# Expert blocks of 128 rows and two lookup tables in a two-layer ViT tower

## What is computed

```python
h = tok(x)                                # patch embedding, 128 x 3 x 224 x 224
h = h + causal_attention(layernorm(h))
h = h + ffn0(layernorm(h))                # top 2 of 32 experts, hidden size 128, relu
h = h + decayed_mix(layernorm(h))
h = h + ffn1(layernorm(h))                # top 2 of 16 experts, hidden size 512, gelu

# ffn0, with w zero except for a token's two chosen experts:
h = relu(einsum('td,edh->teh', xt, keys))
out = einsum('teh,te,ehv->tv', h, w, values)
```

## Time and profile before

| What | us |
|---|---|
| Median of 3 runs | 1412.7 (1410.9 to 1418.58) |
| Profiled execution, its own time | 1420.37 |
| Its span | 1418.6 |
| Front, tables and pads of L0 | 0 to 489 |
| Expert blocks of L0 | 489 to 746 |
| Middle | 746 to 1054 |
| Expert blocks of L1 | 1054 to 1343 |
| End | 1343 to 1418.6 |

### The profile page before, as it was taken

How to read it: one execution, slowest core, us unless ns; L and a number is a source line. 1 busy time by engine, 2 the same in 40 slices (tenths; PEclk the granted TensorE clock), 3 DMA queues, 4 the chain that set the end, 5 groups by cost and what they waited for, 6 DMA issues and landing times.

```text
span 1418.6 us, 23674 instructions
## 1 busy us (share of the span) xinstructions
PE 995.0 (70%) x6272; PEld 821.7 (58%) x6272; DVE 810.1 (57%) x2985; ACT 501.7 (35%) x1416; POOL 707.3 (50%) x698
## 2 busy tenths in 40 slices
PE   5999999999985066666643544444429999999700
PEld 3576666766654055555533444444419999999700
DVE  1577878778775033333325777777625666666433
ACT  1443434434332011111113444444415665665400
POOL 1034535445353267777770566666654555555500
PEclk9999999999985598888865777766659999999955
DMA  9756666566311654444424333333257777777388
GB/s 374 265 196 225 217 231 228 200 231 220 120 40 30 189 156 146 145 142 144 146 61 106 97 96 97 91 91 72 55 162 252 249 241 244 243 248 244 98 240 237
DMA packets 121170, 243.61 MB, mean 172 GB/s; under 512 B 21976, under 2 KB 88603, under 8 KB 114754
## 3 DMA queue, kind: packets, MB, share of 16 engines
q1 hardware_dynamic: 83168, 189.90, 41.3%
q0 software_dynamic: 21504, 34.73, 7.8%
q10 hardware_dynamic: 16458, 18.51, 4.6%
HBM read 188.84 MB, written 60.18 MB: 176 GB/s over the span
## 4 chain that ended last, share of the span: by engine, by line
PE 54%; DMA 13%; DVE 11%; issue 7%; ACT 5%; POOL 5%; SPq 3%; ACTq 0%; DVEq 0%; POOLq 0%
PE ps L654 11%; PE ps L639 8%; PE ps L491 7%; PE ps L488 5%; DMA xin<-resid_L 4%; PE ps L733 4%; POOL results_L L1578 4%; DMA results_L<-xin 4%; DMA xin<-lists_L 3%; PE ps L736 3%; ACT ntok L994 2%; PE ps L552 2%; PE ps L570 2%; PE ps L536 2%; PE ps L624 2%
## 5 line engine op out<-in xcount | busy, mean ns | idle before, releaser
L1565 POOL DMA_INDIRECT lists_L<-rows,slots x320 | 358.3, 1120 | 417.2 <-issue 374.1
L1578 POOL DMA_INDIRECT results_L<-xin x352 | 344.6, 979 | 217.7 <-DVE xin L1384 145.5
L654 PEld LDWEIGHTS ps<-xin,hTb 128*128 128x128 f32 x1664 | 219.7, 200 | 9.2 <-DVE hTb L1353 0.3
L654 PE MATMUL ps<-xin,hTb 128*128 128x128 f32 x1664 | 224.2, 282 | 0.1
L491 PE MATMUL ps<-xin,w_emb 128*128 128x512 f32 x384 | 180.8, 603 | 10.3 <-DMA w_emb<-in_w_main 10.3
L624 PE MATMUL ps<-ident,xin 128*128 128x128 f32 x352 | 82.4, 321 | 131.3 <-DMA xin<-lists_L 130.6
L936 ACT ACTIVATE hTb<-ps,xin 128x256 f32<-128x256 f32 x320 | 125.6, 475 | 107.2 <-PE ps L639 107.2
L1353 DVE TENSOR_SCALAR hTb<-ps 128x256 f32<-128x256 f32 x96 | 40.8, 425 | 174.3 <-PE ps L635 174.3
L733 PE MATMUL ps<-ntok,w_emb 104*104 104x128 f32 x160 | 49.2, 432 | 120.2 <-ACT ntok L994 120.2
L624 PEld LDWEIGHTS ps<-ident,xin 128*128 128x128 f32 x352 | 42.7, 154 | 152.4 <-DMA xin<-lists_L 152.3
L810 ACT ACTIVATE xTb<-ps 128x256 f32<-128x256 f32 x96 | 36.9, 384 | 236.6 <-PE ps L624 236.6
(11 more groups left out here) (187 smaller groups left out, 2015.2 us busy)
## 6 DMA issues: line engine op xcount, KB each, us to landing
xin<-in_x_main SPq DMA_DIRECT2D x48, 1536.0 KB, 8.4
xin<-in_w_L SPq DMA_DIRECT2D x80, 578.0 KB
xin<-lists_L SPq DMA_DIRECT2D x176, 132.0 KB
xin<-results_L SPq DMA_DIRECT2D x32, 520.0 KB
xin<-in_w_L SPq DMA_DIRECT2D x96, 128.0 KB
resid_L<-htok ACTq DMA_DIRECT2D x32, 260.0 KB
xin<-resid_L SPq DMA_DIRECT2D x32, 260.0 KB
results_L<-xin POOLq DMA_INDIRECT x352
```

What stands on the lines that cost most here:

```text
L654: mm = pe.matmul(o, hTb[p2][:, f, q * 128:(q + 1) * 128], w2[:, f * D:(f + 1) * D], start=(f == 0), stop=(f == l.FC - 1))
L1565: pool.indirect_dma_start(out=lists[l.name], out_offset=bass.IndirectOffsetOnAxis(ap=slots[h][:, t, k:k + 1], axis=0), in_=rows[h][:, t, k ...
L1578: pool.indirect_dma_start(out=results[l.name], out_offset=bass.IndirectOffsetOnAxis(ap=xblk[u][:, q, PLACE:PLACE + 1].bitcast(U32), axis=0 ...
```

## The change

Blocks of L0 have 128 rows in place of 256. The number of blocks is no longer rounded up to a multiple of 8: L0 has 161, L1 still 80. `rounds` now runs the first 8 blocks, 18 turns of a loop (blocks 8 to 151) and the last 9 (L1: 8) as straight code, on every engine. The semaphore counts that L1 starts from are kept for each buffer, since buffer 0 is used 21 times in L0 and the others 20 times. In place of `tb.entry` there are two tables, `tb.weights_at` with the first row of the expert's weights and `tb.rows_at` with the first row in the lists; SP loads one number from each and divides nothing. VectorE makes them with one instruction less. The buffers in SBUF are the same 8. With 128 rows a block needs one transpose, one scatter and half the columns in each matmul and each copy; its weights are 128 KB as before, its rows 66 KB.

```diff
-        most = (TOKENS * TOP + experts * (block - 1)) // block
+        self.blocks = (TOKENS * TOP + experts * (block - 1)) // block
         self.unroll = unroll
-        self.blocks = -(-most // unroll) * unroll
+        self.rounds = self.blocks // unroll
+        self.turns = [len(range(u, self.blocks, unroll)) for u in range(unroll)]
-L0 = Layer(1, "L0", 32, 128, 256)
+L0 = Layer(1, "L0", 32, 128, 128)
 L1 = Layer(2, "L1", 16, 512, 256)
@@ rounds
-            for u in range(l.unroll):
-                body(u, 0)
-            with eng.Fori(1, l.blocks // l.unroll) as j:
-                for u in range(l.unroll):
+            U = l.unroll
+            for i in range(U):
+                body(i, 0)
+            with eng.Fori(1, l.rounds - 1) as j:
+                for u in range(U):
                     body(u, j)
+            for i in range(U * (l.rounds - 1), l.blocks):
+                body(i % U, i // U)
@@ load, on SP
                 i = l.unroll * j + u
-                entry = sp.value_load(tb.entry[0:1, bass.ds(i, 1)], min_val=0, max_val=l.E * l.step - 1)
-                e, r = entry // l.step, entry % l.step
-
-                sp.wait_ge(k.y_out[u], k.y0 + 16 * l.Q * j)
-                sp.dma_start(wblk[u][:, 0:l.W], weights[bass.ds(e * 128, 128), :]).then_inc(k.blk_in[u], 16)
+                e = sp.value_load(tb.weights_at[0:1, bass.ds(i, 1)], min_val=0, max_val=(l.E - 1) * 128)
+                r = sp.value_load(tb.rows_at[0:1, bass.ds(i, 1)], min_val=0, max_val=l.E * l.room)
+                sp.wait_ge(k.y_out[u], k.y0[u] + 16 * l.Q * j)
+                sp.dma_start(wblk[u][:, 0:l.W], weights[bass.ds(e, 128), :]).then_inc(k.blk_in[u], 16)
@@ tables, on DVE
-                link(dve.tensor_scalar(tb.ef[:, 0:n], pair[0][0:1, 0:n], float(E - 1), None, ALU.min))
+                link(dve.tensor_scalar(tb.weights_at[:, 0:n], pair[0][0:1, 0:n], float(E - 1), 128.0, ALU.min, ALU.mult))
-                link(dve.tensor_scalar(tb.rf[:, 0:n], tb.rf[:, 0:n], float(E * l.room), None, ALU.min))
-                dve.scalar_tensor_tensor(tb.entry[:, 0:n], tb.ef[:, 0:n], float(l.step), tb.rf[:, 0:n],
-                                         ALU.mult, ALU.add).then_inc(T.tables_ready, 1)
+                dve.tensor_scalar(tb.rows_at[:, 0:n], tb.rf[:, 0:n], float(E * l.room), None, ALU.min)\
+                    .then_inc(T.tables_ready, 1)
```

More of the change, by code:

```diff
@@ L65, in __init__ @@
         self.room = TOKENS + block
-        self.step = experts * self.room + 1
-        most = (TOKENS * TOP + experts * (block - 1)) // block
+        self.blocks = (TOKENS * TOP + experts * (block - 1)) // block
         self.unroll = unroll
-        self.blocks = -(-most // unroll) * unroll
+        self.rounds = self.blocks // unroll
+        self.turns = [len(range(u, self.blocks, unroll)) for u in range(unroll)]
         self.W = 2 * hidden + (self.FC + D if self.FC > 1 else 0)
-L0 = Layer(1, "L0", 32, 128, 256)
+L0 = Layer(1, "L0", 32, 128, 128)
 L1 = Layer(2, "L1", 16, 512, 256)
@@ L118, in __init__ @@
         self.cb, self.ge, self.v = sb("t_cb", [32, 1]), sb("t_ge", [32, 192]), sb("t_v", [32, 2])
-        self.ef, self.rf = sb("t_ef", [1, 192]), sb("t_rf", [1, 192])
-        self.entry = sb("t_entry", [1, 192], I32)
+        self.rf = sb("t_rf", [1, 192])
+        self.weights_at, self.rows_at = sb("t_weights_at", [1, 192], I32), sb("t_rows_at", [1, 192], I32)
         self.fr = sb("t_fr", [1, 32], I32)
@@ L166, with __init__ @@
 class BlockSignals:
-    def __init__(self, sem, i0, j0, y0, first=None):
-        self.i0, self.j0, self.y0 = i0, j0, y0
+    def __init__(self, sem, before=None, first=None):
+        self.i0 = before.blocks if before else 0
+        self.j0 = before.turns if before else [0] * NB
+        self.y0 = [16 * before.Q * j0 if before else 0 for j0 in self.j0]
         if first is None:
@@ L343, in build @@
         S = {l.name: LayerSignals(sem, halves, l.name) for l in (L0, L1)}
-        K = {"L0": BlockSignals(sem, 0, 0, 0)}
-        K["L1"] = BlockSignals(sem, L0.blocks, L0.blocks // NB, 16 * L0.Q * L0.blocks // NB, K["L0"])
+        K = {"L0": BlockSignals(sem)}
+        K["L1"] = BlockSignals(sem, L0, K["L0"])
         m_in = halves("m_in")
@@ L385, in rounds, with beyond @@
         def rounds(eng, l, body):
-            for u in range(l.unroll):
-                body(u, 0)
-            with eng.Fori(1, l.blocks // l.unroll) as j:
-                for u in range(l.unroll):
+            U = l.unroll
[3 more added lines that the diff above has]
+                for u in range(U):
                     body(u, j)
+            for i in range(U * (l.rounds - 1), l.blocks):
+                body(i % U, i // U)
+        def beyond(l, u, j, n):
+            return isinstance(j, int) and l.unroll * j + u + n >= l.blocks
         def pads(eng, l, half):
@@ L452, in _ @@
             for u in range(NB):
-                sp.wait_ge(K["L0"].y_out[u], 16 * L0.Q * L0.blocks // L0.unroll)
+                sp.wait_ge(K["L0"].y_out[u], 16 * L0.Q * L0.turns[u])
             for h in range(2):
@@ L462, in _ @@
             for u in range(NB):
-                sp.wait_ge(K["L1"].y_out[u], K["L1"].y0 + 16 * L1.Q * L1.blocks // L1.unroll)
+                sp.wait_ge(K["L1"].y_out[u], K["L1"].y0[u] + 16 * L1.Q * L1.turns[u])
             for h in range(2):
@@ L621, in t1 @@
                     b, jj = turn(u, n, j)
-                    pe.wait_ge(k.blk_in[b], 32 * (k.j0 + jj + 1))
+                    pe.wait_ge(k.blk_in[b], 32 * (k.j0[b] + jj + 1))
                     for q in range(l.Q):
@@ L659, in i_par @@
                     return (u + n) % 2
-                rounds = l.blocks // U
                 t1(0, 0, 0)
@@ L664, in expert_blocks, with step @@
                 t2(0, 0, 0)
-                def step(u, j, last):
-                    if not (last and u + 2 >= U):
+                def step(u, j):
+                    if not beyond(l, u, j, 2):
                         t1(u, j, 2)
-                    if not (last and u + 1 >= U):
+                    if not beyond(l, u, j, 1):
                         t2(u, j, 1)
                     t3(u, j, 0)
[L672 to L678, removed]
+                rounds(pe, l, step)
             def step(g, h, j, ahead_a, ahead_e):
@@ L942, in high @@
                     i = U * j + u + n
-                    act.wait_ge(k.blk_in[(u + n) % U], 32 * (k.j0 + j + (u + n) // U + 1))
+                    act.wait_ge(k.blk_in[(u + n) % U], 32 * (k.j0[(u + n) % U] + j + (u + n) // U + 1))
                     if not (isinstance(i, int) and i < 2):
@@ L952, in expert_blocks, with step @@
                         f(0, 0, n)
-                for u in range(U):
+                def step(u, j):
                     for f, lead in works:
[L955 to L958, removed]
+                        if not beyond(l, u, j, lead):
                             f(u, j, lead)
[L960 to L963, removed]
+                rounds(act, l, step)
             pads(act, L0, 1)
@@ L1311, in tables @@
                 E, n = l.E, l.blocks
-                st = Steps(9 * (l.turn - 1))
+                st = Steps(8 * (l.turn - 1))
                 def link(ins):
@@ L1332, in tables @@
                 dve.wait_ge(T.tab_ps, l.turn)
-                link(dve.tensor_scalar(tb.ef[:, 0:n], pair[0][0:1, 0:n], float(E - 1), None, ALU.min))
+                link(dve.tensor_scalar(tb.weights_at[:, 0:n], pair[0][0:1, 0:n], float(E - 1), 128.0, ALU.min, ALU.mult))
                 link(dve.scalar_tensor_tensor(tb.rf[:, 0:n], iotaB[0:1, 0:n], float(l.block), pair[1][0:1, 0:n],
                                               ALU.mult, ALU.add))
-                link(dve.tensor_scalar(tb.rf[:, 0:n], tb.rf[:, 0:n], float(E * l.room), None, ALU.min))
-                dve.scalar_tensor_tensor(tb.entry[:, 0:n], tb.ef[:, 0:n], float(l.step), tb.rf[:, 0:n],
-                                         ALU.mult, ALU.add).then_inc(T.tables_ready, 1)
-                assert st.n == 9, st.n
+                dve.tensor_scalar(tb.rows_at[:, 0:n], tb.rf[:, 0:n], float(E * l.room), None, ALU.min)\
+                    .then_inc(T.tables_ready, 1)
+                assert st.n == 8, st.n
             tables(L0)
@@ L1374, in gated @@
                     dve.wait_ge(k.y_ps, k.i0 + i + 1)
-                    dve.wait_ge(k.y_out[u], k.y0 + 16 * l.Q * j)
+                    dve.wait_ge(k.y_out[u], k.y0[u] + 16 * l.Q * j)
                     y = ps[:, 6 + p2, 0:l.Q * D].rearrange("p (q d) -> p q d", q=l.Q)
@@ L1378, in gated @@
                     if l.FC > 1:
-                        dve.tensor_tensor(yblk[u][:, :, :], y,
+                        dve.tensor_tensor(yblk[u][:, 0:l.Q, :], y,
                                           wblk[u][:, None, l.W - D:l.W].to_broadcast([128, l.Q, D]), ALU.add)\
@@ L1382, in gated, with step @@
                         dve.wait_ge(y_biased, i + 1)
-                        y = yblk[u][:, :, :]
```

(8 more changed lines are left out.)

## The result

The changed kernel takes 1558.5 us (median of 4 runs, 1557.2 to 1559.0), the kernel before 1412.3 in the same comparison: 1.102 times as long, 95% interval 1.099 to 1.106, or 146 us more. The profiled execution took 1557.2 us, its span 1555.4.

The account below looks back on a forecast made before the run. POOL's scatters were taken to bind before, SP after: 394.2 us of its issuing and the edges end L0's blocks 143 us later; with 1 us for L1, 144 us on the median 1412.7 give 1557 us (1530 to 1590).

Parts of the forecast that it names:

- What binds before: L0's blocks in the kernel before: POOL's scatters bind at 2.55 us per block, SP second at 1.88.
- (e): SP in L0's blocks: two lookups make 2.48 us per block in the loop, 2.18 in straight code; SP binds, 394.2 us.
- (f): Both ends of L0's blocks: smaller pads let SP start 3 us sooner; tail 9.2 us in place of 19.4.
- (g): L1's 80 blocks: the second lookup fits in SP's waits, except 1 us (0 to 2) at the start.
- The sum: Whole kernel: L0's last results land at 889.0 against 746.0, 143 us later, plus 1 us for L1: 1557 us.
- a sign of being wrong: Outside L0's blocks: the prediction is wrong if the rest of the kernel moves by more than some 3 us.
- (a) to (d): L0's POOL (205.6 us), PE, DVE and ACT, buffer loop (1.3 us per block), transfers (105 GB/s): none binds after.
- The 1.3 us of the loop through a buffer: L0: loading, computing, scattering and reloading a buffer takes 7.9 us, over 6 blocks 1.3 us each; not on the path.
- Rival four: L0's blocks: not slower, SP does not bind; POOL or the buffer loop does at 1.3 us; about 1372 us, chance 3%.
- Overlapping lookups: SP in L0: the second lookup overlaps the first, adding 0.3 us in place of 0.68; about 1498 us, chance 7%.
- Dearer lookups: SP in L0: at 567 ns per load, two loads add 0.58 us per block, 93 us; about 1650 us, chance 6%.
- SP does not bind: Same as Rival four: POOL or the buffer loop sets L0's blocks at 1.3 us; about 1372 us, chance 3%.

Follow-up runs that it names:

- r2: Changed kernel with L0's blocks put back to 256 rows, two tables kept; 1417.1 us against 1414.1 for the kernel before, ratio 1.002.
- r3: Changed kernel (128 rows) with one packed table, one lookup and the division of the kernel before; 1470.2 us, ratio 1.040 to the kernel before.
- r1: The changed kernel itself once more, as the measure for other runs; 1559.9 us against 1414.1 for the kernel before, ratio 1.103.
- r5: Changed kernel with one more lookup per block of L0, its value unused; 1644.5 us against 1416.2 for the kernel before.
- r6: As r4, but ACT issues the weights five blocks ahead in place of four; 1410.7 us against 1416.2 for the kernel before, ratio 0.996.
- r4: Changed kernel, but in L0 ACT looks up and issues the weights; no checks behind block lookups; 1394.4 us against 1414.1 for the kernel before.
- e1: Same kernel as r2 (256 rows, two tables), another run; 1615.4 us against 1596.5 for the kernel before, ratio 1.012.
- e5: Changed kernel with each block of L0 scattering its results a second time, into an unread tensor; 1817.4 us against 1570.0 for the kernel before.
- e6: Same kernel as r4 (ACT issues L0's weights, no checks), another run; 1532.2 us against 1570.0 for the kernel before, ratio 0.974.
- e2: Same kernel as r3 (128 rows, one packed table), another run; 1601.6 us against 1596.5 for the kernel before.
- e3: Same kernel as r5 (one more unused lookup per block of L0), another run; 1763.8 us against 1596.5 for the kernel before.
- e4: Changed kernel without the limit comparison and assertion behind each lookup; 1604.2 us against 1596.5 for the kernel before, ratio 1.006.

## Why the prediction was right

It gave 1557 us (1530 to 1590) and the way of the change; measured are 1558.5. By its steps:

- **What binds before** (POOL, with SP next): right. r2 shows it from the other side: SP's wait fell from 57.4 to 6.1 us, and the time did not fall; it grew by 3 us.
- **(e) SP binds after.** Right, and this is what carried the sum. Second lookup: predicted 0.68 us, in the chain 0.66, in the difference of r3 and r1 90 / 161 = 0.56 with the division in the other direction, so 0.64; by the means of SP's steps, 2.41 and 1.88, it is 0.61. Division: predicted 0.08, found 0.049 + 0.033 = 0.08 (medians of the register work), 0.09 in the chain of r3. The issuing took 387.8 us in place of 393.8 (394.2 less the last issue): 2.43 us for a block in the loop in place of 2.48, and 2.17 in straight code, where I had 2.18. The 1.88 us per block for SP's own work with the old table were right: they are the mean of SP's steps in r3 too, where SP never waits. So the 6 us are in the second lookup, which I had priced 0.04 to 0.07 us too high.
- **(f) the edges.** The gain of 3 us from smaller pads did not come. The last pad landed after 7.18 us in place of 6.51 in one profile, and in that of r1 after 7.21; the first lookup was at 491.8 and 488.7 against 489.0. From the first pad to the first lookup it is 26.5 us before, 26.7 and 26.6 after, and 26.7 in r2, whose pads are of the old size. So the size of the pads does nothing. The other transfer that ran then is ACT's load behind its pads, but no run here took it away, so that is a guess. The late 491.8 comes for the most part from the front of that one profile, where the first pad is issued at 465.1 in place of 462.5. The tail was predicted at 9.2 us and is 9.7. From the landing of the last rows PE, ACT and DVE take 3.3 us, where I had 2; the scatter and the landings were shorter than priced.
- **(g) L1.** Predicted 1 us more; from its first lookup to the first load behind it, it takes 291.7 us before and 292.0 after. Right within what one can see. SP's wait in it fell from the 119.8 us of the earlier trace rows to 77.0, 0.54 us for each of 80 blocks: here too the second lookup came out of a wait.
- **The sum.** From the first lookup or the first load of each stage to that of the next:

| | Before | After | Difference |
|---|---|---|---|
| To the blocks of L0 | 489.0 | 491.8 | 2.8 |
| Blocks of L0 | 257.3 | 397.5 | 140.2 |
| Middle | 307.8 | 306.8 | -1.0 |
| Blocks of L1 | 291.7 | 292.0 | 0.3 |
| End | 72.8 | 67.4 | -5.4 |

The stage was to end at 889.0 and ended at 889.2. Two errors cancel in this: 5.8 us too early a start, 6 us too long an issue. That the end agrees to a fraction of a us is luck. The prediction of 144 us was against the profiled execution, whose span grew by 136.8. The end has nothing of the change in it, yet it moved by 5.4 us, more than the 3 us that I had named as a sign of being wrong. It is the part that varies by itself: with the same code it took 67.0 us in the profile of r2, 67.2 in r5, 71.2 in r6 and 76.5 in r4, whose profile is the slowest of its five runs. So the long end of the profile before is probably the greater part of the 7.7 us by which it lay above the median; there is no second profile of the kernel before to show it. Median against median the change costs 146 us, 2 more than forecast.
- **(a) to (d), what does not bind:** right, POOL idle, the transfers at 102 GB/s against 105. That PE might stand at its lower clock came true (0.50), and cost nothing while SP bound. The 1.3 us of the loop through a buffer were not tested by the changed kernel; where this loop does bind, in r4, it takes 1.4 to 1.6 us, since the landings take about 3 us there. Rival four, which went on at 1.3 us, would have come out too low.
- **The rivals.** Overlapping lookups: refuted by r5. Dearer lookups: no, the median load is 272 ns. SP does not bind: refuted, no wait in 161 blocks. The floor of about 600 ns for a `tensor_load` that the Trainium skill states (DMA: Bandwidth & Descriptors, Latency and other measured facts) does not hold here either: the load itself takes 262 to 455 ns in the changed kernel, and only with address and check does a lookup come to 0.66 us.

## What to carry to other kernels

A block costs its issuing queue a fixed amount however small the block is; when blocks are halved, sum up the queue's own work per block (lookups, checks, register work, issues) against the rate of the engine that binds, before the gain on that engine is counted. A sequencer does not appear among the busy engines: divide the stage less the queue's waits by the blocks, and that is the rate at which it will bind (1.88 us here before, and 1.88 in r3, where it did bind). And work that is free under a wait (here 0.6 us a block with blocks of 256 rows) is paid in full as soon as the wait is gone; a second lookup (0.64 us) in place of a division (0.08 us) is such work.

## What the hardware showed

- A lookup by SP's sequencer is 0.64 to 0.66 us in the loop: address 0.1, load 0.3, comparison and assertion 0.26. A division and a remainder of a register add 0.05 and 0.035 us. An issue of 66, 128 or 132 KB takes 0.33 us itself each, and 0.52 with its register work where nothing is divided.
- The time until a transfer has landed rose from 2.0 us to about 3 (2.4 to 3.2 in the pieces of the chain, the first apart) when the stage's traffic rose from 102 to 171 GB/s (the changed kernel and r4), while the engines of the transfers were busy 0.36 and 0.63 of the time. In r4 the loops through buffers got longer just where they turned faster.
- Instructions of SP's sequencer that take 0.02 to 0.33 us can take 0.7: 111 of them in e1, 146 in e5 and 80 in e6, 18 to 21 in e2, e3 and e4, at most one in r1 to r6. ACT has some too (7 to 22), and VectorE, TensorE and GpSimd have hardly more of them than in the other runs. It is no fixed trait of a chip: e5 and e6 ran on the same chip as r5 and r6. In the blocks of L0 e1 has 86 of them and takes 325 us, where r2 takes 259; e3 has none there, and SP's step is 2.96 us in the mean as in r5 (2.95). The cause is open.
